# A graph network's edge stages: no node work in the last four edge groups, with banks, seeds and two one-hots ahead of the merge

## The reference, cut to what matters

```
def _egnn_conv(x, src, dst, edge_attr, W_msg, W_edge, W_root, b):
    msg = x[src] @ W_msg + edge_attr @ W_edge
    agg = jax.ops.segment_max(msg, dst, num_segments=x.shape[0])
    agg = jnp.where(jnp.isneginf(agg), 0.0, agg)
    return agg + x @ W_root + b
c1 = leaky_relu(_egnn_conv(X, src, dst, edge_attr, W1_msg, W1_edge, W1_root, b1))
c2 = leaky_relu(_egnn_conv(c1, src, dst, edge_attr, W2_msg, W2_edge, W2_root, b2))
return _layernorm(x + c2)
```

## Time and profile before

| what | value |
|---|---|
| median of three runs | 1830.65 us (1825.43 to 1830.79) |
| profiled execution | 1829.84 us |
| its span | 1828.0 us |
| mean granted clock of TensorE | 0.946 |
| busy share PE, DVE, ACT, POOL | 83%, 70%, 58%, 55% |
| edge stage 0, by the chain | to about 522 us |
| merge 0 | 524 to 831 us |
| edge stage 1 | 834 to about 1340 us |
| merge 1 | 1342 to 1828 us |

### The profile page before, as it was taken

The page is one execution under the profiler, slowest core; times in us unless marked ns, Lnnn a source line. Parts: engine busy times, 40 slices in busy tenths (PEclk is TensorE's granted clock), DMA queues, the critical chain, the costliest instruction groups (busy, mean ns, idle before and its releaser), DMA issues.

```text
span 1828.0 us, 36625 instructions
## 1 busy us (share of the span) xinstructions
PE 1518.9 (83%) x11422; PEld 1354.1 (74%) x11422; DVE 1277.1 (70%) x1946; ACT 1068.6 (58%) x2402; POOL 999.1 (55%) x1454
## 2 busy tenths in 40 slices
PE   3999888989899999886999988988987766676664
PEld 2677777878789888885777777777787765675664
DVE  2665555555556555554899888888847888888887
ACT  2355555555534555663555555555538888888887
POOL 6777777777700000005777777777757555454443
PEclk9999999999999999997999999999999889878887
DMA  7769989888856788885888898888969999999997
GB/s 141 210 193 265 272 250 255 250 264 258 250 199 197 249 267 283 285 273 168 241 259 250 258 243 253 263 253 235 257 205 279 296 296 284 292 293 297 281 281 202
DMA packets 505019, 459.10 MB, mean 251 GB/s; under 512 B 348553, under 2 KB 412340, under 8 KB 504836
## 3 DMA queue, kind: packets, MB, share of 16 engines
q1 hardware_dynamic: 444118, 321.15, 62.2%
q0 software_dynamic: 30976, 57.72, 13.1%
q10 hardware_dynamic: 29742, 77.88, 10.9%
HBM read 283.25 MB, written 173.37 MB: 250 GB/s over the span
## 4 chain that ended last, share of the span: by engine, by line
PE 31%; POOL 30%; DMA 15%; issue 13%; ACT 7%; DVE 3%; SPq 1%; ACTq 0%; POOLq 0%; DVEq 0%
POOL arena_hold L419 28%; PE ps L597 20%; DMA out_dram<-arena_hold 7%; PE ps L508 4%; DMA arena_hold<-nodes,src_perm 4%; ACT arena_hold L776 3%; DMA arena_hold<-in_x_dram,src_all 3%; POOL onehot L454 2%; PE ps L474 2%; ACT ps L700 2%; PE ps L499 2%; ACT arena_hold L722 2%; PE ps L467 2%; DVE stats L1000 1%; DVE ps L983 1%
## 5 line engine op out<-in xcount | busy, mean ns | idle before, releaser
L597 PE MATMUL ps<-arena_hold,onehot 128*128 x4688 | 616.5, 295 | 166.5 <-POOL onehot L454 132.9
L597 PEld LDWEIGHTS ps<-arena_hold,onehot 128*128 128x128 f32 x4688 | 590.2, 208 | 193.1 <-issue 192.1
L419 POOL DMA_INDIRECT arena_hold<-nodes,src_perm x392 | 370.6, 945 | 448.7 <-SPq L384 329.5
L508 PEld LDWEIGHTS ps<-w_root,onehot 97*128 97x128 f32 x3136 | 399.1, 193 | 100.5 <-issue 97.0
L419 POOL DMA_INDIRECT arena_hold<-in_x_dram,src_all x392 | 377.2, 962 | 125.0 <-issue 115.5
L508 PE MATMUL ps<-w_root,onehot 97*128 97x128 f32 x3136 | 415.3, 275 | 0.0
L920 DVE TENSOR_TENSOR_SCAN arena_hold<-keep,arena_hold,ps 96x512 f32<-96x512 bf16 x196 | 248.5, 1268 | 209.1 <-PE ps L474 208.0
L661 ACT COPY arena_hold<-ps 128x384 f32<-128x384 f32 x392 | 187.9, 479 | 273.4 <-PE ps L508 270.5
L454 POOL CAST onehot<-keep 128x256 f32<-128x256 uint8 x588 | 209.6, 410 | 204.1 <-ACT ps L700 144.6
L934 DVE TENSOR_TENSOR onehot<-count,rel 128x1024 f32<-128x1024 bf16 x147 | 179.5, 1222 | 127.2 <-PE ps L597 123.2
L499 PE MATMUL ps<-ident,arena_hold 128*96 128x128 f32 x1568 | 240.8, 277 | 0.0
(11 more groups left out here) (97 smaller groups left out, 1147.1 us busy)
## 6 DMA issues: line engine op xcount, KB each, us to landing
root<-arena_hold ACTq DMA_DIRECT2D x196, 384.0 KB
arena_hold<-root SPq DMA_DIRECT2D x196, 384.0 KB, 4.0
nodes<-arena_hold SPq DMA_DIRECT2D x98, 384.0 KB, 3.0
arena_hold<-nodes SPq DMA_DIRECT2D x98, 384.0 KB
arena_hold<-in_x_dram SPq DMA_DIRECT2D x97, 384.0 KB
arena_hold<-in_x_dram SPq DMA_DIRECT2D x48, 768.0 KB, 9.1
out_dram<-arena_hold SPq DMA_DIRECT2D x48, 768.0 KB, 6.6
onehot_bytes<-arena_hold SPq DMA_DIRECT2D x147, 128.0 KB
```

The lines of the kernel that those rows point to most:

```text
L419: nc.gpsimd.indirect_dma_start(out=gathered[t.ring][0:t.p, i, 0:D], out_offset=None, in_=table_in, in_offset=bass.IndirectOffsetOnAxis(ap= ...
L508: last = nc.tensor.matmul(no_ps[m % 2][:, i * P:(i + 1) * P], nodes_t[m % NODE_RING][0:D + 1, i * P:(i + 1) * P], w_root[0:D + 1, layer * ...
L597: nc.tensor.matmul(ps_bytes[:, bass.ds(place_at, SLOT)].bitcast(F32), onehot[:, k % NS, i, :], rows_from(t)[:, bass.ds(word, SLOT)].bitcas ...
```

## The change

It does six things. The node groups are spread over all edge groups but the last four of a stage. In these last four, once all root products are read, TensorE writes banks 0 to 3 and ScalarE seeds them (before it reads the transposes of the last edge group). In layer 0 VectorE makes the first two one-hot batches before the scan of the last edge group. The byte buffers become three, the byte batches of layer 0 end two groups before the end of the stage, and SP's last byte stores of layer 0 come behind the loads of the first four units of `root`. The PSUM banks get other uses, so that 0 to 3 are those of the node work. `stats` and `small` move into memory of `src_all`.

```
+NODES_OFF = 4
+EARLY = 4
+BYTE_RING = 3
-BYTES_OFF = 8
+BYTES_OFF = (2, 8)
...
-        et_ps, nt_ps, no_ps, em_ps, eb_ps = bank[0], bank[2:4], bank[4:6], (bank[1], bank[6]), bank[7]
+        et_ps, nt_ps, no_ps, em_ps, eb_ps = bank[4], bank[0:2], bank[2:4], (bank[5], bank[6]), bank[7]
...
             if layer:
-                return range(g * NG // NE, (g + 1) * NG // NE)
-            span = NE - TABLES_TAKE
+                span = NE - NODES_OFF
+                return range(min(g * NG // span, NG), min((g + 1) * NG // span, NG))
+            span = NE - TABLES_TAKE - NODES_OFF
...
-            return range(at * NG // span, after * NG // span)
+            return range(min(at * NG // span, NG), min(after * NG // span, NG))
...
-            first, after = (BYTES_AT, NE) if layer == 0 else (BYTES_ON, NE - BYTES_OFF)
+            first, after = (BYTES_AT, NE - BYTES_OFF[0]) if layer == 0 else (BYTES_ON, NE - BYTES_OFF[1])
...
             edge_phase(0)
-            for s in range(4):
-                load_roots(0, s)
+            load_roots(0, 0)
+            load_roots(0, 1)
+            for g in range(NE - EDGE_RING, NE):
+                for k in byte_batches(0, g):
+                    store_bytes(k)
+            load_roots(0, 2)
+            load_roots(0, 3)
...
                     if not groups:
                         messages(t)
+                        nodes_done = rooted == NG
+                        while turned_n == NG and rooted < NG:
+                            root_of(layer, rooted)
+                            rooted += 1
                         if g:
                             turn_back(EdgeGroup(layer, g - 1))
+                        if nodes_done and not primed_early:
+                            pe.wait_ge(root_read, (layer + 1) * NG)
+                            prime(0, EARLY)
+                            primed_early = True
...
-                while rooted < NG:
-                    root_of(layer, rooted)
-                    rooted += 1
-                prime(0, 4)
+                assert rooted == NG and primed_early
+                prime(EARLY, 6)
                 turn_back(EdgeGroup(layer, NE - 1))
-                pe.wait_ge(root_read, (layer + 1) * NG)
-                prime(4, 7)
+                prime(6, 7)
                 pe.wait_ge(held, (layer + 1) * NE)
                 prime(7, 8)
...
                     before = rooted
+                    if g + 1 == NE - 1:
+                        for n in range(EARLY):
+                            act.wait_ge(primed, layer * RING + n + 1)
+                            seed(layer, n)
                     if g + 1 < NE:
                         read_edges(EdgeGroup(layer, g + 1))
+                    while taken == NG and rooted < NG:
+                        read_root(layer, rooted)
+                        rooted += 1
...
             def first_seeds(layer):
-                for n in range(RING):
+                for n in range(EARLY, RING):
...
             def make_bytes(k):
-                if k >= 2:
-                    dve.wait_ge(bytes_stored[k % 2], DMA * (k // 2))
-                compare(bytes_out[:, k % 2, :].rearrange("p (t n) -> p t n", n=P), k, count_ps).then_inc(bytes_made, 1)
+                if k >= BYTE_RING:
+                    dve.wait_ge(bytes_stored[k % BYTE_RING], DMA * (k // BYTE_RING))
+                compare(bytes_out[:, k % BYTE_RING, :].rearrange("p (t n) -> p t n", n=P), k, count_ps).then_inc(bytes_made, 1)
...
+                    if layer == 0 and g == NE - 1:
+                        dve.wait_ge(no_full, NG)
+                        one_hots(0, NS)
                     scan(EdgeGroup(layer, g))
                     if g:
                         hold_chunks(EdgeGroup(layer, g - 1))
...
-            one_hots()
+            one_hots(NS, NBATCH)
```

More of the change, by code:

```diff
@@ L107, in gnn @@
         src_all = sb("src_all", [P, NE * C], I32)
+        STATS, SMALL = RI // 2 * 6, 5 * RI
+        spare = src_all[:].bitcast(F32)
+        stats = spare[:, 0:STATS].rearrange("p (j c) -> p j c", c=6)
+        small = spare[:, STATS:STATS + SMALL].rearrange("p (i j) -> p i j", j=RI)
         src_perm = sb("src_perm", [P, NE * C], I32)
@@ L262, in gnn @@
         dev, inv, shift = small[:, 0, :], [small[:, 1 + i, :] for i in range(2)], [small[:, 3 + i, :] for i in range(2)]
-        both = stats[:].rearrange("p j (h c) -> p j h c", c=3)
+        both = stats.rearrange("p j (h c) -> p j h c", c=3)
         mean, spread = both[:, :, :, 1], both[:, :, :, 2]
@@ L385, in _ @@
             edge_phase(1)
-            for i in range(2):
-                sp.wait_ge(bytes_stored[i], DMA * ((NBATCH + 1 - i) // 2))
+            for i in range(BYTE_RING):
+                sp.wait_ge(bytes_stored[i], DMA * ((NBATCH + BYTE_RING - 1 - i) // BYTE_RING))
             load_roots(1, 0)
@@ L438, in _ @@
                 gather(EdgeGroup(1, g))
-            for i in range(2):
-                pool.wait_ge(bytes_stored[i], DMA * ((NBATCH + 1 - i) // 2))
+            for i in range(BYTE_RING):
+                pool.wait_ge(bytes_stored[i], DMA * ((NBATCH + BYTE_RING - 1 - i) // BYTE_RING))
             pool.wait_ge(scanned, 2 * NE - 2)
@@ L524, in tables @@
                         if stage == 0:
-                            last = nc.tensor.matmul(bank[2 + i][:, 0:n], placed[0:kp, k * P:(k + 1) * P], pick[k][0:kp, at:at + n],
+                            last = nc.tensor.matmul(bank[i][:, 0:n], placed[0:kp, k * P:(k + 1) * P], pick[k][0:kp, at:at + n],
                                                     start=k == 0, stop=k == KT - 1)
                         else:
-                            last = nc.tensor.matmul(bank[2 + i][0:1, 0:n], number_f[0:kp, k:k + 1], pick[k][0:kp, at:at + n],
+                            last = nc.tensor.matmul(bank[i][0:1, 0:n], number_f[0:kp, k:k + 1], pick[k][0:kp, at:at + n],
                                                     start=k == 0, stop=k == KT - 1)
@@ L533, in tables @@
                         kp = P if k < KT - 1 else LEFT_CH
-                        last = nc.tensor.matmul(bank[5][0:1, 0:2 * NSB], ones[0:kp, :], done_by[k][0:kp, :], start=k == 0, stop=k == KT - 1)
+                        last = nc.tensor.matmul(bank[3][0:1, 0:2 * NSB], ones[0:kp, :], done_by[k][0:kp, :], start=k == 0, stop=k == KT - 1)
                     last.then_inc(merged, 1)
@@ L860, in piece_rel @@
                     n = min(512, T - at)
[L861 to L862 removed]
+                    nc.vector.tensor_tensor(rel[:, at:at + n], bank[i][:, 0:n], steps_128[:, at:at + n], ALU.subtract)
+                then(nc.vector.tensor_tensor(end_row[0:1, :], bank[3][0:1, 0:2 * NSB], block_end[0:1, :], ALU.add))
                 nc.vector.tensor_scalar(end_words[:], end_row[0:1, :], 1.0, float(T), ALU.add, ALU.min).then_inc(merged_off, 1)
@@ L868, in piece_chunks @@
                     n = min(512, TP - at)
-                    last = nc.vector.tensor_copy(chunk_row[0:1, at:at + n], bank[2 + i][0:1, 0:n])
+                    last = nc.vector.tensor_copy(chunk_row[0:1, at:at + n], bank[i][0:1, 0:n])
                 last.then_inc(merged_off, 1)
@@ L967, in edge_phase, with one_hots @@
                 hold_chunks(EdgeGroup(layer, NE - 1))
-            def one_hots():
-                for k in range(NBATCH):
+            def one_hots(first, after):
+                for k in range(first, after):
                     dve.wait_ge(seeded[0], dve.value_load(open_words[0:1, k:k + 1], min_val=1, max_val=NG))
```

24 lines of the change are left out of this document (6 added, 18 removed).

## The result

The changed kernel takes 1813.95 us (median of 5 runs, 1810.20 to 1817.44) against 1830.65 (5 runs, 1823.19 to 1830.79): ratio 0.9926, 95% interval 0.9908 to 0.9944. The profiled execution took 1810.2 us (span 1808.4). The kernel before had medians of 1827.49 to 1828.45 us in four later series of 12 to 23 runs, so 1830.65 was a high one and about 14 us is the better figure.

What follows compares the result with a forecast made beforehand. Gathers on POOL were taken to set the pace of both edge stages, TensorE alone their ends. The terms 3.5 + 4.65 - 0.6 gave 7.55 us, so 1823.1 us against the median of 1830.65; range 1818.5 to 1828.5.

Steps and rivals of the forecast that it cites:

- walk, stage 0: End of edge stage 0, TensorE's turn of group 97 to last bank: 9.45 us instead of 12.97, gain 3.5.
- walk, stage 1: End of edge stage 1, TensorE's turn of group 97 to last bank: 7.09 us instead of 11.75, gain 4.65.
- last bank to both merges: From the last bank written to the first merge matmul, both stages: stays 2.4 us, so no gain.
- last gather later, both: Gathers of group 97: land 0.3 us later in each stage, taking 0.6 us off the gain.
- merge 0 and merge 1 by themselves: Length of the two merges: no change forecast, only their starts move, so 0 us.
- Pace: Gathers of both edge stages: stay at 1.25 us each with node work in fewer groups, costed at nothing.
- The tails: End of both edge stages, turn of group 97 to last bank: 9.45 and 7.09 us at TensorE's lower clock.
- the rival of the clock that holds: Ends of both edge stages run at 2.4 GHz: 10.4 us gained, 1820.2 us; chance 0.10.
- I take this 2.4 us as fixed: Between last bank and merge only the load of 16 words stands: 2.4 us, so merges start with the last bank.
- the rival: Last gathers land 2.5 us later in each stage beside root loads: 3.1 us gained, 1827.5 us; chance 0.23.
- One-hots, seeds, banks: Stage ends: early seeds hide in the gather wait, cost nothing; two one-hots delay stage 0's last scan, 2.36 us.
- Both merges follow their start: Both merges and edge stage 1: move with their start, so the whole 7.55 us gain reaches the end.

Runs made afterwards that it cites:

- nodes_off_12: The changed kernel with no node work in the last 12 edge groups of a stage instead of the last four: 1814.47 us, ratio 0.9916 to the kernel before.
- the old order: The kernel before, profiled twice (1826.2 us in the second run), and the kernel before with only `stats`, `small` and the byte area placed anew (1825.26 us).
- Nodes off only: The changed kernel with no banks, seeds or one-hots made early, node work still out of the last four groups: 1812.79 us, ratio 0.9921 to the kernel before.
- roots_late: Nodes off only, with SyncE waiting for TensorE's turn of group 97 before any root load in either stage: 1810.08 us, ratio 0.9901 to the kernel before.
- start_0_held: The changed kernel with 24 extra matmuls of 512 columns holding the start of merge 0: 1825.33 us, ratio 0.9987 to the kernel before.
- start_1_held: The changed kernel with 24 extra matmuls of 512 columns holding the start of merge 1: 1827.08 us, ratio 0.9991 to the kernel before.

## Why the prediction was off

| term of the sum | forecast | measured (means of the table) |
|---|---|---|
| walk, stage 0 | 3.5 | 4.2 |
| walk, stage 1 | 4.65 | 5.0 |
| last bank to both merges | 0 | 2.0 |
| last gather later, both | -0.6 | -1.8 |
| merge 0 and merge 1 by themselves | 0 | 0.6 and 3.9 |
| sum | 7.55 | 13.9 |

*Pace: right.* It cost nothing, and nodes_off_12 shows three times the margin that was needed.

*The tails: right in place and nearly in size.* 9.45 and 7.09 us were forecast; 9.15 and 8.42, 5.72 and 7.57 were measured. The clock was the unsure part, as said: over the walk of stage 0 the granted clock was 0.70 and 0.75, over that of stage 1 0.98 and 0.50, so the rival of the clock that holds came true in part of the executions.

*The step that failed: "I take this 2.4 us as fixed".* What stands between the last bank and the merge is what the prediction named, the load of 16 words; but its length is not fixed. The chain of waits of the kernel before does not show the load. It goes through the first one-hot, in stage 1 through the first four casts, and calls the rest "issue" (start, us, what):

```profile
522.21 1.24 DVE onehot L934
523.45 0.80 issue
524.25 5.77 PE ps L597 x28
...
1339.22 1.45 POOL onehot L454 x4
1340.67 1.19 issue
1341.86 3.34 PE ps L597 x14
```

The load has a row of its own, on TensorE's sequencer (PEldq: shortest, median and longest ns, then first and last start in us). The first two lines are the kernel before, in stages 0 and 1, the other two the changed kernel:

```profile
L580 PEldq TENSOR_LOAD <-rows x1: 2192/2192/2192, 521.8 to 521.8; - x1
...
L580 PEldq TENSOR_LOAD <-rows x1: 2262/2262/2262, 1339.4 to 1339.4; - x1
...
L593 PEldq TENSOR_LOAD <-rows x1: 1293/1293/1293, 518.3 to 518.3; - x1
...
L593 PEldq TENSOR_LOAD <-rows x1: 1258/1258/1258, 1328.9 to 1328.9; - x1
```

In all of these the load starts with the last bank, and the first matmul of the merge follows its end by 0.2 us, whatever the one-hots and casts do: in the kernel before they had ended 0.8 and 1.2 us ahead of that matmul. In the three profiles of the old order the six loads took 1.59 to 2.82 us (means 2.20 and 2.33), in the two of the changed kernel 1.25 to 1.29. The differences, 0.9 and 1.1 us, are the 2.0 us that the step gave where 0 was forecast. *Nodes off only*, with nothing early, has the short load too (1.30 and 1.24 us), so it does not come from early banks, seeds or one-hots; it came with the rest of the change, and the node work that leaves the tail is the likely part, not run apart. The early one-hots add 0.3 us in stage 0: without them the first one-hot ends last there, 0.19 us before the merge. Why the load is longer behind a tail with node work stays open. Busy transfers alone are not the reason: it took 2.19 us at a DMA share of 1.05 in the kernel before, and 1.29 us at 1.06 in roots_late.

*The last gather: right sign, too small.* 0.3 us was taken near the first bound; 1.0 and 0.8 were measured at the turn. The mechanism is that of the rival: in the changed kernel, beside root loads, group 97 is turned 5.4 to 5.9 us after the last gather was issued, and 3.1 to 3.3 us after it with these held back. Only part of this was lost, because TensorE before came to group 97 no sooner than 4.4 us after the issue. The Trainium skill ("DMA: Bandwidth & Descriptors", "Queues, rings and completion order") has each DMA engine go round its queues packet by packet; by that, loads on SyncE's queue take turns away from the gathers of POOL's, and roots_late agrees.

*One-hots, seeds, banks: right.* They are hidden in the wait or buy nothing that can be measured, and the early one-hots do delay the last scan. What the third byte buffer and the earlier byte batches do by themselves was not tried apart from the rest.

*"Both merges follow their start": right, and the second step that failed.* Holding the starts shows it for both. But the prediction put a change in the merges' own length at nothing, and in the table that term, 0.6 and 3.9 us, is the largest miss. Merge 1 was shorter in itself: 478.1 to 483.8 us in eleven profiles of kernels with the node work out and no hold (mean 480.5), 481.4 to 486.1 in three of the old order (mean 483.1). Transfers in flight at its start, and the time at which root loads leave, are spoken against by one profile each above. Profiles of one kernel differ by up to 4.7 us in that stretch (486.1 and 481.4), so part of the 3.9 us in the table is scatter; the means of all profiles differ by 2.6, an estimate of what is real. Its cause stays open.

## What to carry to other kernels

A stage whose pace is set by one engine still ends on another: count what stands on the other engines after the last item of the pace-setter, and move that into earlier items, if there is room as there was here. When a step looks fixed, or a chain calls it issue, look for the sequencer's own row in it, and read that row in more than one profile: here the same load of 16 words took 1.25 to 2.82 us. Loads that are brought forward run beside the last transfers of the stage before and delay them (here by 2.7 us and more at the turn), so try holding back those that nobody needs yet; in the total that was too little to tell here.

## What the runs showed of the hardware

- 24 matmuls of 512 columns with one row of weights, back to back, took 10.42 us in stage 0 of start_0_held (0.43 us each, granted clock 0.50, so 1.2 GHz throughout), and the 64 matmuls of the merge behind them 9.48. In stage 1 of start_1_held 24 took 9.17 us; the granted clock was 0.65 in the first half and 0.50 in the second, so it fell while TensorE was busy with them.
- A load of 16 words into TensorE's registers took 1.12 us in the median over merge 0 of the kernel before (73 loads behind the first, 0.91 to 2.06 us). Behind the last bank it took 1.25 to 1.29 us in the changed kernel and 1.59 to 2.82 us in the old order. With it moved ahead, 0.54 us remain between the last write of a bank and the merge in stage 0.
- An indirect gather of 84 rows was there for TensorE at most 3.1 us after its issue with no root load in flight (roots_late) and 5.9 us after it behind four loads of 384 KB (nodes_off_only), in the same stage of kernels that are otherwise alike.
